# A decoder layer on one core: constants ahead of the input, the similarity chain among the value tiles, and probability-times-value rounds of two key tiles together

## The reference

```python
x = _layernorm(x + _L0_attn_ref(x, ...))                   # layer 1: 16 heads of 32, gated
x = _layernorm(x + _L0_xattn_ref(x, ctx_1024, ctx_1024, mask, ...))   # layer 2: 16 heads of 32, masked
x = _layernorm(x + _L0_ffn_ref(x, sim_matrix, gates, ...)) # layer 3: 16 experts, routed, causal

# layer 1
attn = softmax(inner @ outer.T / sqrt(dh)) * aperture[..., :, None] * expression[..., None, :]
attn = attn / (attn.sum(-1) + 1e-8);  out = rotated_and_scaled(attn @ v) @ Wout
# layer 2
scores = where(mask == 0, -1e9, q @ k.T / sqrt(32));  out = (softmax(scores) @ v) @ Wo.T + bo
# layer 3, gating
logits = _normalize(x) @ _normalize(sim_matrix) - sigmoid(gates)
```

## Time and profile before

| | |
|---|---|
| median of 3 executions | 4212.06 us (4207.79 to 4214.97) |
| the profiled execution | 4212.77 us, span 4211.0 us, granted clock 0.982 |
| PE busy | 3986.5 us, 95% of the span |
| ACT, DVE, POOL busy | 1683.9 us, 2441.0 us, 1705.1 us |
| opening, to the first step of the pairs | 126.2 us |
| pairs of layer 1, of layer 2, one section | 272 to 288 us, 302 us |

### The profile page before, as it was taken

How to read it: one execution, slowest core, us unless ns; L and a number is a source line. 1 busy time by engine, 2 the same in 40 slices (tenths; PEclk the granted TensorE clock), 3 DMA queues, 4 the chain that set the end, 5 groups by cost and what they waited for, 6 DMA issues and landing times. The chain is left out here.

```text
span 4211.0 us, 56965 instructions
## 1 busy us (share of the span) xinstructions
PE 3986.5 (95%) x20456; PEld 2319.8 (55%) x20456; DVE 2441.0 (58%) x4051; ACT 1683.9 (40%) x3098; POOL 1705.1 (40%) x1187
## 2 busy tenths in 40 slices
PE   6999999999999998999899989998998799999998
PEld 5443744554374446444644464446443688888886
DVE  4563466355455636674667466746673766666664
ACT  2454255335525543443344334433444322222322
POOL 0212221321212233775377537753763344444443
PEclk9999999999999999999999999999999899999998
DMA  3321332142224335223422342234222200000000
GB/s 103 74 64 51 94 74 61 57 113 55 54 79 97 84 99 145 51 69 123 120 51 69 122 121 51 69 118 118 47 49 68 105 31 31 31 31 30 24 31 13
DMA packets 175561, 303.55 MB, mean 72 GB/s; under 512 B 55280, under 2 KB 73200, under 8 KB 175280
## 3 DMA queue, kind: packets, MB, share of 16 engines
q1 hardware_dynamic: 164784, 282.60, 25.0%
q10 hardware_dynamic: 10496, 17.31, 1.2%
HBM read 154.06 MB, written 43.77 MB: 47 GB/s over the span
## 5 line engine op out<-in xcount | busy, mean ns | idle before, releaser
L1129 ACT ACTIVATE probs_a<-half_a 128x512 f32<-128x512 f32 x2048 | 1123.8, 595 | 999.8 <-PE half_a L965 458.1
L962 PE MATMUL half_a<-stack_a 97*128 97x512 f32 x2048 | 862.7, 479 | 37.3 <-ACT probs_a L1129 25.9
L1368 DVE TENSOR_REDUCE mx_a<-wide_a 128x1 f32<-128x1024 f32 x512 | 605.8, 1220 | 433.8 <-PE wide_a L918 430.1
L1364 DVE CUSTOM_DVE_ANT_0 wide_a<-wide_a,mask_q_a 128x1024 f32<-128x1024 f32 x512 | 620.3, 1245 | 313.1 <-PE wide_a L918 308.2
L918 PE MATMUL wide_a<-stack_a 96*128 96x512 f32 x2048 | 665.8, 430 | 30.6 <-DVE mx_a L1364 11.9
L962 PEld LDWEIGHTS half_a<-stack_a 97*128 97x128 f32 x2048 | 376.0, 193 | 570.1 <-ACT probs_a L1129 331.7
L812 POOL TENSOR_TENSOR psums_a<-psums_a,probs_a 128x1024 f32<-128x1024 f32 x232 | 561.1, 2438 | 126.5 <-ACT probs_a L1129 111.5
L901 PE MATMUL acc_a<-probs_a,v_a 128*32 128x512 f32 x4096 | 553.8, 612 | 2.5 <-ACT u_a L1114 2.3
L918 PEld LDWEIGHTS wide_a<-stack_a 96*128 96x128 f32 x2048 | 377.6, 192 | 205.8 <-issue 83.4
L965 PE MATMUL half_a<-mask_k_a,eye_a 128*128 128x512 fp8e5 x1024 | 407.9, 398 | 0.0
L1680 POOL TENSOR_TENSOR weighted_e<-weighted_e 128x512 f32<-128x512 f32 (+2 forms) x288 | 241.4, 838 | 222.5 <-DVEq L1908 188.3
(11 more groups left out here) (298 smaller groups left out, 4895.1 us busy)
## 6 DMA issues: line engine op xcount, KB each, us to landing
stack_a<-qk_a SPq DMA_DIRECT2D x336, 256.0 KB, 4.5
y_a<-x SPq DMA_DIRECT2D x8, 2048.0 KB, 8.9
x<-y_a SPq DMA_DIRECT2D x8, 2048.0 KB, 10.9
mstage_a<-mask SPq DMA_DIRECT2D x32, 512.0 KB, 4.2
mstage_a<-mask_t SPq DMA_DIRECT2D x32, 512.0 KB, 3.8
den_a<-denominators SPq DMA_DIRECT2D x252, 64.0 KB, 2.0
stack_a<-first_a SPq DMA_DIRECT2D x48, 256.0 KB, 5.1
stage_a<-x_t SPq DMA_DIRECT2D x20, 512.0 KB, 3.7
```

Of the source, the lines that this page charges most:

```text
L962: last = pe.matmul(bank[:, :], stack[0:3 * DH + 1, s, 2 + h, kt * P:(kt + 1) * P], stack[0:3 * DH + 1, s, h, c * CH:(c + 1) * CH], start=T ...
L1129: act.activation(probs[:, kt % 2 * 2 + h, c * CH:(c + 1) * CH], bank[:, :], ACT.Exp, scale=SCALE).then_inc(free, 1)
L1364: dve.tensor_tensor_reduce(bank[:, :], bank[:, :], mask_q[:, t, :], 1.0, -3e38, ALU.add, ALU.max, mx[:, p % 3, n:n + 1]).then_inc(free, 1)
L1368: dve.tensor_reduce(mx[:, p % 3, n:n + 1], bank[:, :], AX.X, ALU.max).then_inc(free, 1)
```

## The change

Three edits.

1. SP issues seven constants first, then `xk`, then similarity and gates, then `wv` and `wk`, and four constants that only layer 2 needs last, on a semaphore of their own (`late_in`), for which POOL, ACT and DVE wait after section 0. The splits of `wv` stand ahead of the gate steps.
2. The similarity chain is cut in four steps, put behind the value tiles 0, 1, 3 and 6.
3. In pairs 1 to 4 of layer 1 and 1 to 5 of layer 2, odd steps have no `pv`, and even steps have those of two tiles. `probs` gets a third slot (`third`), in a region of `first`. The first loads of the mask move from step 0 of pair 6 to step 4, with waits for the third slot, and the split of `wv` waits for it in layer 1.

```diff
+COUPLED = (5 * TT, 6 * TT)
+def prob_slot(att, n):
+    if TT <= n < COUPLED[att]:
+        return n % 3
+    return (n + 1) % 2 if att == 0 and n >= TT else n % 2
+def rounds_after(att, p, kt):
+    n = p * TT + kt
+    if n < TT or n > COUPLED[att]:
+        tiles = [n - 1]
+    else:
+        tiles = [] if kt % 2 else [n - 1] if n == TT else [n - 2, n - 1]
+    return [divmod(m, TT) for m in tiles if m >= 0]
...
-            parts = block_parts(att, *before) if before[0] >= 0 else ()
+            rounds = [("pv", *tile, part) for tile in rounds_after(att, p, kt) for part in block_parts(att, *tile)]
...
-            steps += [("pv", *before, part) for part in parts] + late
+            steps += rounds + late
...
-                if nxt:
-                    steps += [("mload", 0), ("mload", 1)]
+            if nxt == 1 and kt == 4 and p == 6:
+                steps += [("mload", 0), ("mload", 1)]
...
-        steps += [("split", "xk", k) for k in range(KT)] + [("EX", 0), ("EX", 1), ("split", "wv", 0), ("split", "wv", 1)]
+        steps += [("split", "xk", k) for k in range(KT)] + [("split", "wv", 0), ("split", "wv", 1), ("EX", 0), ("EX", 1)]
...
+            for n, t in enumerate((0, 1, 3, 6)):
+                tail[t].append(("sim", n))
...
+        third = sb("third", [P, 2, S], at=place["first"])
...
-        CONSTS = 11
+        CONSTS = 7
+        LATE_CONSTS = 4
...
+                        if k == 0 and what == "wv" and sec.att == 0 and sec.nxt == 0:
+                            pool.wait_ge(pv_done, blocks.upto(sec, final(sec, 4, TT - 1)))
...
-            pe.wait_ge(norm_sem, 1)
-            for k in range(KT):
-                last = pe.matmul(wides[0][:, 0:E], all_ones[:, :], sim_sq[:, k, :], start=(k == 0), stop=(k == KT - 1))
-            last.then_inc(norm_sem, 1)
-            pe.wait_ge(norm_sem, 3)
...
-                        if h == 0 and c == 0 and n >= 2:
-                            old = ((n - 2) // TT, (n - 2) % TT)
+                        if h == 0 and c == 0 and n == TT and sec.att == 0 and stores.before(sec):
+                            act.wait_ge(xt_stored[0], stores.before(sec) * 16)
+                        elif h == 0 and c == 0 and n >= 2 and n != TT:
+                            old = divmod(max(m for m in range(n) if prob_slot(sec.att, m) == prob_slot(sec.att, n)), TT)
```

More of the change, by code:

```diff
@@ L91, in pair_steps @@
             due = [("mneg", m[1]) for m in units_ if m[2:] == (1, TT - 1)]
-            parts = block_parts(att, *before) if before[0] >= 0 else ()
+            rounds = [("pv", *tile, part) for tile in rounds_after(att, p, kt) for part in block_parts(att, *tile)]
             if not rate:
-                steps += [("pv", *before, part) for part in parts[:1]]
-                parts = parts[1:]
+                steps += rounds[:1]
+                rounds = rounds[1:]
             if rate == 3:
@@ L467, in layers @@
         const_in = sem("const_in")
+        late_in = sem("late_in")
         sim_in = sem("sim_in")
@@ L528, in chunk_parts, with prob @@
             return half(0), half(1)
+        def prob(sec, p, kt, h):
+            slot = prob_slot(sec.att, p * TT + kt)
+            return third[:, h, :] if slot == 2 else probs[:, 2 * slot + h, :]
         def wide_unit(eng, sec, step):
@@ L588, in _ @@
                              allow_slow_non_contiguous=True).then_inc(const_in, 16)
[L589 to L593, removed]
+            for k in range(KT):
+                sp.dma_start(raws["xk"][:, k, :], own["kv_src"][0:1, k * P:(k + 1) * P, :].rearrange("b p s -> (b p) s"))\
+                  .then_inc(direct_in["xk"][k], 16)
+            sp.dma_start(sim_raw[:, :, :], experts_io["sim"].rearrange("(k p) e -> p k e", p=P)).then_inc(sim_in, 16)
+            sp.dma_start(e_gates[:, :], experts_io["gates"].partition_broadcast(P)).then_inc(sim_in, 16)
             for what in ("wv", "wk"):
@@ L598, in _ @@
                       .then_inc(direct_in[what][k], 16)
+            for t, name in ((bq, "bq"), (bk, "bk")):
+                sp.dma_start(t[:, :], late[name].rearrange("(g p) -> p g", p=P),
+                             allow_slow_non_contiguous=True).then_inc(late_in, 16)
+            for t, name in ((bv, "bv"), (bo, "bo")):
+                sp.dma_start(t[:, :], late[name].partition_broadcast(P)).then_inc(late_in, 16)
             sp.wait_ge(setup, 2)
@@ L840, in run @@
                         pool.drain().then_inc(ct_split, 1)
-            for plan in plans:
+            run(plans[0])
+            pool.wait_ge(late_in, 16 * LATE_CONSTS)
+            for plan in plans[1:]:
                 run(plan)
@@ L876, in run @@
                     kind = step[0]
+                    if step == ("sim", 0):
+                        pe.wait_ge(norm_sem, 1)
+                        for k in range(KT):
+                            last = pe.matmul(wides[0][:, 0:E], all_ones[:, :], sim_sq[:, k, :], start=(k == 0),
+                                             stop=(k == KT - 1))
+                        last.then_inc(norm_sem, 1)
+                        continue
+                    if step == ("sim", 3):
+                        pe.wait_ge(norm_sem, 3)
+                        continue
                     if kind == "pv":
@@ L1163, in run @@
                         act.drain().then_inc(turn_sem, 1)
-                        act.activation(warm[:, :], eye[:, 0:1], ACT.Exp)
-            for plan in plans:
+                    elif step == ("sim", 2):
+                        act.wait_ge(norm_sem, 3)
+                        act.activation(norm[:, 1, :], norm[:, 0, :], ACT.Sqrt)
+                        act.drain()
+                        act.activation(norm[:, 2, :], e_gates[:, :], ACT.Exp, scale=-1.0)
+                        act.drain().then_inc(norm_sem, 1)
+            run(plans[0])
+            act.wait_ge(late_in, 16 * LATE_CONSTS)
+            for plan in plans[1:]:
                 run(plan)
@@ L1419, in run @@
                         turn_weights(step[1])
+                    elif kind == "sim":
+                        similarity(step[1])
                     elif kind == "out":
@@ L1451, in run @@
                         layer_norm(range(HALF + 2 * n, HALF + 2 * n + 2))
-            for plan in plans:
+            run(plans[0])
+            dve.wait_ge(late_in, 16 * LATE_CONSTS)
+            for plan in plans[1:]:
                 run(plan)
```

67 lines of the change are left out of this document (31 added, 36 removed).

## The result

| | before | after |
|---|---|---|
| median | 4216.38 us (4207.79 to 4229.85, 16 executions) | 4235.56 us (4223.29 to 4249.6, 16 executions) |
| profiled execution, span | 4211.0 us | 4240.4 us |
| first step of the pairs, after the span's start | 126.2 us | 120.8 us |
| the eight sections of pairs, layer 1 / layer 2 | 1087.0 / 1208.8 us | 1126.0 / 1203.7 us |

The ratio is 1.0043, 95% interval 1.0034 to 1.0053: the change makes the kernel 18 us slower (14 to 22). The forecast was +11. The two profiled executions differ by 29 us, of which layer 1 has +39.0, layer 2 -5.1 and the opening -5.4.

A forecast was written before the change was run, and what follows sets the result against it. TensorE, busy 95% of the span, was taken to bound the kernel. Layer 1 +33, layer 2 -8 and opening -14 sum to +11 on a median of 4212.1, so about 4223 us; range 4197 to 4243.

The forecast's parts named there:

- the opening moves by less than 10: Start of the kernel: a stated sign that the forecast is wrong, as is a move of more than 17; -14 us was forecast.
- Layer 1: Pairs 1 to 4: bank waits exceed saved turns, +0.60 a plain double step, 8.3 a section, +33 us in four batches.
- last of pair 4: Layer 1's last double step there: three maxima units per step give cover, waits are gone, saving stands, -0.4.
- The turn: TensorE going from full-array matmuls to column tiles and back: 0.38 lost per turn in layer 1, 0.32 in layer 2.
- the 0.62 of the walk: Layer 1 plain double step: first st waits 0.62 for ACT's Exp, the next 0.25, restart 0.10; sum 0.97.
- Layer 2: Pairs 1 to 5: +0.18 a plain double step, offset by relief from POOL; -2.1 a section, -8 us in four batches.
- POOL's relief: Layer 2, step 4 of pairs 1 to 4: with three slots Exp waits for an older add, and 0.56 comes back.
- The opening: Start of the kernel: earlier xk, gates and value tiles, partly given back at the similarity sums; -14 us, ends -10 and -16.
- SP now reaches it some 4 earlier: Opening: SP issues the last turn load some 4 earlier, so it lands at 31.7 instead of 35.6.
- The bank wait is small: Rival, chance 0.18: layer 1's plain double-step wait is 0.60 or under, giving 4204, or 4191 at 0.4.
- POOL gives no relief: Rival, chance 0.12: layer 2's Exp still waits on queued adds, so layer 2 costs +14 and the time is 4246.
- The opening gives half: Rival, chance 0.10: clock falls to 1.2 GHz after value tile 0, tiles 1 and 2 take 5 more, giving 4228.

The follow-up runs named there:

- x_l1: Layer 1's two-tile coupled rounds and third slot alone, opening and layer 2 as before, against the kernel before: 4250.67 us, ratio 1.0095.
- x_l1_spread: Layer 1 alone coupled, with head 1's scores between the two maxima units, against the kernel before: 4272.31 us, ratio 1.0127.
- x_l1_exp: Layer 1 alone coupled, exponentials of its pairs 1 to 5 on 256 of 512 columns, against the kernel before: 4233.58 us, ratio 1.0048.
- x_turns: Kernel before, nothing coupled, with one more turn per step in pairs 1 to 4 of layer 1: 4232.58 us, ratio 1.0034.
- x_slot2: Third slot in layer 2 alone, nothing coupled, against the kernel before: 4207.33 us, ratio 0.9982.
- x_open: The new opening alone, pairs uncoupled with two slots, against the kernel before: 4211.83 us, ratio 0.9992.
- x_open2: New opening alone, with the four late constants issued behind the turn loads, against the kernel before: 4210.66 us, ratio 0.9992.
- x_open3: New opening alone, four late constants behind the turn loads and each turn step one value tile later, against the kernel before: 4204.15 us, ratio 0.9965.
- x_l2: Layer 2's two-tile coupled rounds and third slot alone, opening and layer 1 as before, against the kernel before: 4203.66 us, ratio 0.9978.
- x_l2_spread: Layer 2 alone coupled with third slot, head 1's scores between the two maxima units, against the kernel before: 4183.81 us, ratio 0.9914.
- x_best: Layer 1 uncoupled, layer 2 with third slot, coupled and spread, opening with late constants and turn steps moved, against the kernel before: 4167.12 us, ratio 0.9888.

## Why the prediction was right, and where not

**The number is in part luck, and one of the prediction's own signs says wrong.** The range of 4197 to 4243 holds the 4235.56, the forecast's own 4219 to 4228 does not, and the change is +18 where +11 was forecast. "The forecast is wrong if ... the opening moves by less than 10": it moved by 3 in the medians and by 5.4 in the profile. So the account of the opening failed, and the sum came near because the whole cost 9 less than its three parts do.

**Layer 1: direction and walk right; a cost beside the walk was missed.** Forecast +33, measured +40 (33 to 47) by x_l1. Step by step:

| double step | before | forecast | after |
|---|---|---|---|
| plain | 7.91 | 8.51 | 8.47 |
| with the copy to `u` | 8.44 | 8.88 | 8.78 |
| maxima turned, into the next pair | 8.76 | 9.46 | 9.42 |
| last of pair 4 | 9.97 | 9.6 | 10.5 |

By the measured steps a section loses 8 x 0.56 + 4 x 0.34 + 3 x 0.66 + 0.5 = 8.3, the 8.3 of the forecast; four make 33. The one row with the wrong sign is the last: with three maxima units a tile the half banks are covered, but the units of two tiles now follow each other on the two wide banks, and TensorE waits 0.53 for DVE there (at 547.08). The small misses of the others make up for it. Stretches at half the clock come on top, for which the prediction had no term in layer 1. This is one in the changed kernel; the columns are the stretch, its length, busy time and instructions of PE, PEld, DVE, ACT and POOL, the granted clock, DMA share and GB/s:

```profile
177.00:183.80 6.80, 6.55 (x29) 2.16 (x32) 2.63 (x3) 1.08 (x2) 2.53 (x2) 0.53 0.17 40
183.80:190.60 6.80, 6.39 (x36) 3.21 (x32) 3.81 (x4) 4.16 (x8) 0.00 (x0) 1.00 0.00 0
```

and PE, then DVE and POOL, ahead of it:

```profile
174.17 0.98 PE L1001 MATMUL half_a<-stack_a 97*128 97x512 f32 x2 [0.41 <-ACT third_a L1165]
176.20 0.88 PE L957 MATMUL wide_a<-stack_a 96*128 96x512 f32 x2 [1.05 <-DVE mx_a L1417]
177.33 1.22 PE L957 MATMUL wide_a<-stack_a 96*128 96x512 f32 x2 [0.25 <-DVE mx_a L1417]
...
171.87 2.35 DVE L1461 TENSOR_TENSOR thin_a<-thin_a,over_thin_a 128x16 f32<-128x16 f32 x1 [2.32 <-DMA thin_a<-u_a]
...
171.80 2.38 POOL L771 TENSOR_TENSOR qk_a<-k_raw_a,qk_a 128x1024 fp32r<-128x1024 f32 x1
```

TensorE waited for a bank and then for DVE, which had been held 2.35 by one small operation (see the last section); from 176.6 the clock is at the lower level (1.2 GHz) for 6.8 us, 0.53 on average over the first stretch shown, and the double step takes 4.9 more. In pairs 1 to 4 of layer 1 the changed kernel has three such stretches (about 11 us together), x_l1 two (6), x_l1_spread four, x_l1_exp one. The ten profiled executions in which these pairs are not coupled have none. So coupling leaves TensorE idle by 0.4 to 1.6 us at places where it was not, and now and then the clock goes down behind it. The 33 are shown step by step; that the rest of the +40 is the clock is not. The profiled executions of x_l1 and before differ by 38, but only 30 of it lies between the first and last `st` of layer 1's sections: 33 and 6 on one side, and against them time that before itself lost in its first section (9.10 and 12.65 in two double steps that take 7.91 and 9.60 where nothing disturbs them). The other 8 lie where the two kernels are the same.

**The turn: 0.38 was too much as the price of the turn itself** (0.26 by x_turns), but not as a term of the sum. In the trace after, the wait is the 0.62 of the walk, and the pair of `st` behind it takes 0.35 more than two matmuls, the 0.25 and 0.10 of the walk. With 0.97 of waits and a double step longer by 0.56, one turn fewer gave back 0.41.

**Layer 2: right in sum.** Forecast -8 (-2.1 a section), measured -9 (-13 to -5), and -1.8 by the shortest sections (188.2 to 186.4). Plain 8.11 (forecast 8.13). POOL's relief was 0.57 per step 4 (forecast 0.56), and x_slot2 has it alone. Wrong in detail: one of the steps from pair to pair got longer (11.24 to 11.85, forecast -0.5), and in pair 5 the double step (5, 6) got 2.3 shorter (11.71 to 9.41) where I had nothing; these misses partly offset others of the walk.

**The opening: the gain was 9 to 11 us smaller than forecast.** Forecast -14, measured -3 (-7 to 0) by x_open; in the profiles the pairs begin 5.4 (the change) and 6.5 (x_open) earlier. EX at 16.05 (forecast 15.8) and value tile 0 at 26.7 (27.3) were right. The step "SP now reaches it some 4 earlier" was wrong: I took SP's four idle us for a wait that goes away, and issues of 0.5 for a constant cost. In fact single issues from the tenth us on take 2.4 to 3.9 us here and there, whatever stands there (3.91 at `bv`, 2.58 at `Wout`; in x_open2 2.37 at `Wi`, 3.01 at `Wout_swapped`, 2.44 at `beta_p`), so the last turn load was issued at 31.1 instead of 24.5, and had landed at 37.0. What stood behind it on DVE, the squares of the similarity matrix, had become part of TensorE's path by the change. Of the 9.2 by which the profile's 5.4 falls short of the walk's 14.6 (48.6 - 34), this late load is 5.3 (39.33 for 34); another 3.4 are the halved clock in tiles 1 and 7, which the prediction had in a rival only (5, for tiles 1 and 2). The -14 was there to be had: x_open3 shows it.

**The rivals.** "The bank wait is small" is refuted by the 0.62 between 213.57 and 214.19. "POOL gives no relief" is refuted by x_slot2. "The opening gives half" came true in direction: the opening gave less than half, the clock was the smaller part of it and the DMA the larger. The number, 4223, is 12.6 under the median of after; 4.3 of it is the median of before, 4212.06 in three executions and 4216.38 in sixteen. By the parts alone the misses are 11 in the opening, 7 in layer 1 and -1 in layer 2, 17 in all, against 7 in the whole; the difference is the 9 us by which the three parts sum above the whole (with rounding), which stays open. So does why x_open's medians give 3 where its profile's pairs begin 6.5 earlier.

## What to carry to other kernels

Work that looks like overhead between two uses of a bank (here the rounds of `pv` between the scores of one tile and the next) may be the cover for the engine that empties it. Before two such groups are joined, count the banks that every consumer holds, not just the nearest: when ACT's wait was halved, DVE's took its place. Where the unit of other work between two uses of a ring is long enough, as in layer 2, the joined order with the units spread was the fastest measured (7.74 for a double step, 7.95 before); in layer 1, where 0.93 of work stands against starts 1.2 apart, it was the slowest. And a small step that is moved onto the critical engine's path brings along all that stands ahead of it on its own engine's queue, a DMA wait above all: move it ahead of that, not just to a place that looks free.

## What was not expected of the hardware

- The issue of a DMA by SP is not a fixed cost: the same two loads of `Wi` took 0.88 in the kernel before and 3.50 in x_open2, and a single one up to 3.91 (`bv`, 12.14, in the changed kernel). With the old opening, in the profiles of before and x_l1, no single issue up to the last turn load takes more than 1.6, but SP stands idle for 3.7 us (12.73 to 16.42 in before). With the constants first it is not idle, and two or three issues between 10 and 20 us take 1.8 to 3.9 each. The last turn load is issued at 28.5 in before and at 31.1, 30.2, 29.0, 29.1 and 28.5 in the five profiles with the new order: in none of them did the idle time turn into an earlier load. Which resource is full was not measured.
- A DVE operation on 128x16 elements took 2.35 us at 171.87 where its neighbours take 0.17 to 0.25; of the 32 of its line the median is 0.175 and the longest 2.346. It begins 0.07 after a POOL operation of 2.38 over SBUF and ends with it (174.22 and 174.18). Another of 2.40, at 563.43 on DVE, lies in the same way over one of POOL at 563.41 (2.39), and a halved stretch follows there too, at 569.2. The Trainium skill, SBUF — State Buffer, section "SBUF: two separate sides", states that the two engines share a pair of ports as an exclusive lock for the whole instruction; the traces agree. The kernel before has the same pairing (DVE 2.23 at 177.44, POOL 2.40 at 177.24) and loses by it too, but less:

```profile
181.66 0.74 PE L918 MATMUL wide_a<-stack_a 96*128 96x512 f32 x2 [0.31 <-DVE mx_a L1368]
182.79 0.73 PE L918 MATMUL wide_a<-stack_a 96*128 96x512 f32 x2 [0.40 <-DVE mx_a L1368]
```

Its double step is 9.10 there and not 7.91, with no halved stretch behind it; the changed kernel's is 13.34 and not 8.47.
- There are ten stretches of halved clock in layer 1's coupled pairs, over four kernels, against none in ten profiled executions without coupling. Each begins within 2 us of the end of a wait of TensorE of 0.72 us or more (the wait of 1.05 that ends at 176.20 and the fall at 176.6 in after, 1.59 at 981.54 and 982.5 in x_l1_spread). Other waits of that size have no such stretch behind them, so the runs show the neighbourhood and not a rule.
- In layer 2 it is the other way round. At the end of pair 5 the ten profiled executions without coupling there have 28 such stretches, two to four in each, and the four with coupling (after, x_l2, x_l2_spread, x_best) none. PE of before, then of after, where it turns maxima in that place:

```profile
1884.65 0.38 PE L926 MATMUL wide_a<-neg_eye_a,mm_a 128*16 128x128 f32 x2 [2.53 <-DVE mm_a L1219]
...
1918.40 0.38 PE L965 MATMUL wide_a<-neg_eye_a,mm_a 128*16 128x128 f32 x2 [0.36 <-DVE mm_a L1268]
```

In the changed kernel the rounds of `pv` of two tiles stand ahead of this point (three of them, from 1915.25), in the kernel before one round (from 1881.05), so TensorE has more to do while DVE finishes. So in these profiles coupling brought halved stretches where it made waits, and left none where it covered one. In layer 2 that is about 1.5 us for a stretch (4.6 for the three of before), and it is not the slot that removes them: x_slot2 still has three.
